# A graph network layer stack on one core: adjacency masks built by source tile and place, and the first projection by node tile

## The chip, the cores and the metric

The kernel runs on one core of a Trainium2 chip. Its time is the device time of one execution in microseconds (us). A core has a matrix engine (TensorE, PE), whose weight loads are listed apart as PEld, a vector engine (VectorE, DVE), a scalar engine (ScalarE, ACT), a general engine (GpSimd, POOL) and SyncE (SP), which here only starts transfers. Each engine runs its own instructions in their order and waits on semaphores for the others.

## The reference

1250 nodes with 768 features and 40000 edges, sorted by destination. Two layers; each adds a graph network, a linear attention and a feed-forward block to x. Cut to what this case touches:

```python
edge_index = jnp.stack([src, dst])
xn = _layernorm(x, axis=-1)
x = x + _L0_gnn_ref(xn, edge_index, ...) + _L0_mix_ref(xn[None], ...)[0]     # first layer
# in _L0_gnn_ref, gat_layer, 8 heads of 96, then 1 head of 768
h = (x @ W).reshape(n, heads, out_c)
e = leaky_relu(al_s[src] + al_d[dst], 0.2)            # softmax per destination over its edges
out = segment_sum(h[src] * alpha[:, :, None], dst)
# in _L1_gnn_ref, per convolution
deg = segment_sum(ew, col) + 1.0
norm = rsqrt(deg)[row] * ew * rsqrt(deg)[col]
agg = segment_sum(norm[:, None] * x[row], col)
```

The kernel holds the graph as two dense matrices with the source node on partitions (ten tiles of 125 nodes) and the destination node along a row: `CT` counts the edges from source to destination, and `WA` sums their weights, with ones on its diagonal.

## The kernel before

**Building the adjacency.** The edges lie 128 to a column, 313 columns. Since they are sorted by destination, eight columns (a block, 1024 edges) fall into a window of `WIN` = 38 destinations. For each of the `NB` = 40 blocks VectorE writes a mask of destinations (`destinations`, L1709: a 128x304 comparison, eight columns of 38; L1715: three products of it with the thirds of the edge weight, which is split into three bf16 numbers), the window numbers of the next block (`next_block`, L1728), and for seven of the eight columns a mask of all 1250 sources (`sources`, L1724, a 128x1250 comparison in fp16). ScalarE makes the eighth column's mask by two activations (`source`, L1344, L1346). TensorE multiplies (L906): for each column ten matmuls, one a source tile, of 152 columns (four kinds, count and three weight thirds, by 38). Blocks alternate between two halves of PSUM. ScalarE copies a finished block to SBUF (`stage_block`, L1356, L1358), and GpSimd adds it into `CT` and `WA` (`unstage`, L765 to L772, four 125x380 additions). The position of the window is read from memory into a register (`value_load`). Should an edge lie outside its window, another branch runs (`flag`); the data of this case never takes it.

**Ahead of it** GpSimd fills constants, clears `CT` (L747) and `WA` (L748), and sets the diagonal (L751). VectorE turns the edge numbers into floats (L1662), splits the weights and finds the windows (L1666 to L1703).

**After it** comes a stretch whose order counts for this change:

- VectorE: all statistics of the first LayerNorm (`layer_norm`, L1753), one addition, a wait for ScalarE's square root (L1378), then ten 125x768 normalisations (L1765), each counted on `ln_xn`.
- TensorE: the turns of all ten tiles (`transposes`, L947), then the projection `h1` of all ten (`token_major`, L955, 24 matmuls a tile), the degrees (`deg`, L989), the turned counts (`neg`, L998), then the projections `mk` and `mv` of the attention (L955 again).
- ScalarE: copies the ten turned tiles and then the ten of `h1` out of PSUM (L1335).
- SP: waits for all ten `ln_xn`, loads W2 (L533), waits for the adjacency (`adj_all`), writes `WA` to HBM (L586, L587), waits for `deg_sum`, then loads further weights.
- GpSimd: waits until `WA` is in HBM (`spill`), then sums its ten tiles in place (L786) and counts `deg_sum`, for which TensorE waits ahead of `deg`.
- VectorE, after the LayerNorm: the attention logits of each `h1` tile (`logits`, L1823, L1827), the degrees (L1867), thirty evacuations of `neg` (L1876), and during `mk` and `mv` the feature maps and segment maxima.

**Then** TensorE turns the softmax shifts (`gT`, packet `("gT", 1)`, L980), GpSimd sends them through HBM to all partitions (`drow`, L800, L782), ScalarE takes exponentials of them (`exponentials`, L1452, L1453), VectorE weighs them (`weigh`), and TensorE aggregates (L1055). Twelve query products (`query`, L972) of the attention are worked in between, three of them directly behind `gT`.

The order is written out by hand; `make_plan` numbers the PSUM packets (`take`, `give`, `emptied`), which go round four slots.

## Time and profile before

| | us |
|---|---|
| median of three runs | 3043.74 |
| the three runs | 3042.24, 3043.74, 3043.88 |
| the profiled execution | 3041.95 |
| its span | 3040.2 |
| TensorE busy in the span | 2772.0 (91%) |
| VectorE busy | 1598.3 (53%) |
| ScalarE busy | 949.1 (31%) |
| GpSimd busy | 326.5 (11%) |

All times in the rows are counted from the start of the span; 1.75 us of the profiled execution lie around it. TensorE's clock is given as the granted share of 2.4 GHz: 1.00 is 2.4 GHz, 0.50 is 1.2 GHz.

### The profile page before, as it was taken

Reading aid. Unit: us, or ns where it says so; the run is one execution under the profiler, and the core shown is the slowest. Engines: PE = TensorE matmul, PEld = TensorE weight load, DVE = VectorE, ACT = ScalarE, POOL = GpSimd, SP = SyncE. Lnnn points to the kernel's source line nnn. Section 1 sums busy time; section 2 is a strip of 40 time slices with the busy share of each in tenths; the row PEclk is TensorE's granted clock in tenths of the full one; section 3 lists DMA queues with packets and bytes.
Section 4 is the critical chain, followed back from the end, with each engine's and each line's share of the span. In section 5 each row is a group of like instructions: output and inputs, shape, how many; then the busy total and the mean of one; then the engine's idle time right before and its main releaser. Section 6 shows DMA issues by size and latency. Waiting matters only on the chain.

```text
span 3040.2 us, 33707 instructions
## 1 busy us (share of the span) xinstructions
PE 2772.0 (91%) x13517; PEld 1947.5 (64%) x13517; DVE 1598.3 (53%) x2213; ACT 949.1 (31%) x1081; POOL 326.5 (11%) x315
## 2 busy tenths in 40 slices
PE   4777799999989989969994999999799999899999
PEld 4777665578886656657772675556477777555555
DVE  8999788979994264421115211023376767322220
ACT  3666410048771142211111111013344444322210
POOL 5666330000000001100003000000000000000000
PEclk9999999999999999989996999999899999999999
DMA  9800232121103301177765610000201010200000
GB/s 244 290 0 0 81 80 71 67 83 50 35 18 67 71 23 31 53 245 249 268 230 112 126 52 16 31 0 14 69 28 28 28 42 16 109 10 11 11 11 10
DMA packets 123620, 226.61 MB, mean 75 GB/s; under 512 B 18535, under 2 KB 91788, under 8 KB 123006
## 3 DMA queue, kind: packets, MB, share of 16 engines
q1 hardware_dynamic: 107746, 178.79, 19.8%
q0 software_dynamic: 15760, 46.20, 4.9%
q8 instruction: 84, 1.38, 0.2%
q14 instruction: 30, 0.25, 0.0%
HBM read 158.92 MB, written 66.01 MB: 74 GB/s over the span
## 4 chain that ended last, share of the span: by engine, by line
PE 73%; DVE 17%; issue 3%; DMA 3%; ACT 1%; DVEq 1%; POOL 0%; SPq 0%; ACTq 0%; POOLq 0%
PE ps L955 20%; PE ps L1323 14%; PE ps L1307 13%; DVE arena L1724 6%; PE ps L1145 4%; PE ps L1179 4%; PE ps L1191 4%; PE ps L972 3%; DVE arena L1854 2%; DVE arena L1855 2%; PE ps L1244 1%; PE ps L1055 1%; DVE arena L1823 1%; PE ps L1233 1%; PE ps L1260 1%
## 5 line engine op out<-in xcount | busy, mean ns | idle before, releaser
L955 PE MATMUL ps<-arena 128*125 128x384 f32 x2160 | 712.1, 490 | 9.6 <-issue 6.1
L955 PEld LDWEIGHTS ps<-arena 128*125 128x125 f32 x2160 | 406.4, 190 | 296.2 <-issue 18.8
L1323 PE MATMUL ps<-arena 128*125 128x384 f32 x1280 | 414.6, 487 | 14.3 <-DVE arena L2232 14.3
L1307 PE MATMUL ps<-arena 128*128 128x312 f32 (+1 forms) x1536 | 407.5, 428 | 15.0 <-DVE arena L2232 15.0
L1307 PEld LDWEIGHTS ps<-arena 128*128 128x128 f32 x1536 | 292.4, 190 | 129.9 <-issue 16.9
L1323 PEld LDWEIGHTS ps<-arena 128*125 128x125 f32 x1280 | 240.9, 188 | 187.9 <-issue 16.3
L1335 ACT ACTIVATE arena<-ps 128x750 f32<-128x750 f32 (+4 forms) x145 | 111.6, 786 | 648.5 <-PE ps L955 206.3
L906 PE MATMUL ps<-arena 128*125 128x152 bf16 x3200 | 243.4, 232 | 67.7 <-DVE arena L1724 66.8
L2232 DVE SCALAR_TENSOR_TENSOR arena<-arena 128x1250 f32<-128x1250 f32 (+1 forms) x170 | 231.4, 1383 | 114.8 <-PE ps L1307 111.2
L906 PEld LDWEIGHTS ps<-arena 128*125 128x125 f16 x3200 | 220.9, 137 | 90.1 <-DVE arena L1724 89.1
L1724 DVE TENSOR_SCALAR arena<-arena 128x1250 f16<-128x1250 f16 x280 | 218.2, 851 | 0.0
L1791 DVE SCALAR_TENSOR_TENSOR arena<-ps,arena 125x768 f32<-125x768 f32 x30 | 28.7, 956 | 352.7 <-PE ps L1323 291.7
L1055 PE MATMUL ps<-arena 125*125 125x97 f32 x1600 | 184.1, 277 | 4.8 <-DVE arena L1855 4.8
L1055 PEld LDWEIGHTS ps<-arena 125*125 125x125 f32 x1600 | 182.4, 193 | 7.7 <-DVE arena L1855 5.9
L2144 DVE TENSOR_TENSOR arena<-ps,arena 128x768 f32<-128x768 f32 x34 | 32.6, 958 | 269.5 <-PE ps L1191 269.5
L1847 DVE CUSTOM_DVE_ANT_0 arena<-arena 125x1250 bf16<-125x1250 bf16 x90 | 131.4, 1460 | 23.8 <-DMA arena<-al_src 21.2
L972 PE MATMUL ps<-arena 128*128 128x312 f32 (+5 forms) x496 | 137.0, 436 | 2.1 <-ACT arena L1335 1.1
L1145 PE MATMUL ps<-arena 125*125 125x385 f32 (+1 forms) x400 | 135.3, 494 | 2.8 <-DVE arena L2039 2.8
L1179 PE MATMUL ps<-arena 128*128 128x256 f32 x612 | 134.9, 379 | 1.1 <-ACT arena L1335 1.1
L1191 PE MATMUL ps<-arena 128*128 128x384 f32 x408 | 134.5, 486 | 0.8 <-ACT arena L1335 0.8
L1179 PEld LDWEIGHTS ps<-arena 128*128 128x128 f32 x612 | 116.2, 190 | 20.6 <-issue 1.5
L1452 ACT ACTIVATE arena<-arena,small 125x1250 f32<-125x1250 f32 x80 | 106.8, 1335 | 56.1 <-DVE arena L1855 28.7
(313 smaller groups left out, 2894.5 us busy)
## 6 DMA issues: line engine op xcount, KB each, us to landing
arena<-in_L_ffn_W_dram SPq DMA_DIRECT2D x34, 1152.0 KB, 6.6
xs_rows<-arena SPq DMA_DIRECT2D x1, 30720.0 KB, 100.2
arena<-xs_rows SPq DMA_DIRECT2D x17, 768.0 KB, 7.8
y_rows<-arena POOLq DMA_DIRECT2D x34, 384.0 KB, 3.1
arena<-in_kw_dram SPq DMA_DIRECT2D x24, 512.0 KB, 5.3
arena<-al_dst POOLq DMA_DIRECT2D x18, 625.0 KB, 5.1
arena<-in_kw_dram SPq DMA_DIRECT2D x6, 1536.0 KB, 9.9
arena<-in_x_dram SPq DMA_DIRECT2D x2, 3600.0 KB
```

The lines of the kernel that those rows point to most:

```text
L906: mm = pe.matmul(bank(par, j // 3)[:, o:o + KINDS * WIN], oh_src[:, s, j * TILE:j * TILE + TILE], oh_dst[:, par, u, :, :], start=(fresh an ...
L955: mm = pe.matmul(slot(g)[0:TILE, 512 * half:512 * half + HALF], xt[:, k, i * TILE:i * TILE + TILE], w[:, k, :], start=(k == 0), stop=(k == ...
L972: mm = pe.matmul(slot(g)[0:rows, 512 * b:512 * b + w], stat, mov[:, lo + b * w:lo + b * w + w], start=(t == 0), stop=(t == len(terms) - 1))
L1055: mm = pe.matmul(slot(g)[0:TILE, 512 * (j // 5) + 97 * (j % 5):512 * (j // 5) + 97 * (j % 5) + 97], AT[m % AHEAD][:, j * TILE:j * TILE + T ...
L1145: mm = pe.matmul(slot(g)[0:TILE, 512 * b:512 * b + w], AT2[i][:, j * TILE:j * TILE + TILE], H769[:, i, lo:lo + w], start=(i == 0), stop=(i ...
L1179: mm = pe.matmul(slot(g)[:, 0:TAU], w1s[t % 2][:, k, f * P:f * P + P], xsT[t % 2][:, k, :], start=(k == 0), stop=(k == KT - 1))
L1191: mm = pe.matmul(slot(g)[:, 512 * b:512 * b + HALF], hTt[t % 2][:, f, h * P:h * P + P], w2s[t % 2][:, f, b * HALF:b * HALF + HALF], start= ...
L1307: mm = pe.matmul(slot(g)[:, 512 * b:512 * b + wd_], w[:, r % 2, ORDER[p], o * P:o * P + P], feat[place(f)][:, lo + b * wd_:lo + b * wd_ + ...
L1323: mm = pe.matmul(slot(g)[0:TILE, 512 * b:512 * b + HALF], fv[:, q, :], w2c[m][q][:, b * HALF:b * HALF + HALF], start=(p == 0 and q == 0), ...
L1724: dve.tensor_scalar(oh_src[:, u % RING, :], iota_src, src_c[:, bass.ds(col + u, 1)], None, ALU.is_equal).then_inc(ev("src_hot"), 1)
L1847: chain(dve.tensor_tensor_reduce(out=scratch, in0=neg[:, j, :], in1=row[0:TILE], scale=1.0, scalar=-3.0e38, op0=ALU.add, op1=ALU.max, accu ...
L2232: return dve.scalar_tensor_tensor(out=out_, in0=in_, scalar=edge, in1=of, op0=op, op1=ALU.mult)
```

## The change

**The adjacency.** A source number is split into its tile (`group`, 0 to 9) and its place in it (`member`, 0 to 124). The two masks are now one of 125 places and one of `SPOTS` = 380 spots (tile times 38 plus the offset of the destination in its window). For each block of eight columns VectorE compares the places (128x8x125), multiplies the mask by the first weight third, adds the block before the last from PSUM into `CT` and `WA` (`add_block`, two 125x10x38 additions), and compares the spots (eight 128x380 comparisons). ScalarE multiplies the place mask by the other two thirds (16 activations of 128x125, the weight as scale). TensorE runs four matmuls of 380 columns a column of edges, 32 a block, where it ran 80 of 152. Blocks go round four parts of PSUM. GpSimd has no part in it. The clearing of `WA` goes from GpSimd to ScalarE.

**The stretch after it** goes by node tile: VectorE's statistics and normalisation of one tile follow each other; TensorE turns tile i and then projects tile i-1; ScalarE takes root and turn of tile i+1, then copies `h1` of tile i. SP's and GpSimd's orders stay.

**The shifts.** `gT` is turned behind the first query product, ahead of the second and third.

```diff
-    transposes("xn")
-    token_major("h1", ("gW1", 0), ("gW1", 1))
+    a, b = piece("gW1", 0), piece("gW1", 1)
+    for i in range(NT):
+        packet("T", "xn", i)
+        if i >= 1:
+            packet("h1", i - 1)
+    packet("h1", NT - 1)
...
             own.step(pool.memset(ct_r[0:TILE, 0:6400], 0.0))
-            own.step(pool.memset(aa_r[0:TILE, :], 0.0))
             own.settle()
+            pool.wait_ge(ev("zeroed"), 1)
             for i in range(NT):
                 own.step(pool.tensor_copy(WA[:, i, i * TILE:i * TILE + TILE], ident[0:TILE, 0:TILE]))
             own.settle()
...
+                for u in range(SPREAD):
+                    pe.wait_ge(ev("hot"), n * SPREAD + (u + 1))
+                    pe.wait_ge(ev("hot_act"), n * SPREAD + (u + 1))
+                    for k in range(KINDS):
+                        mm = pe.matmul(bank(s, min(k, 1)), oh_src[:, par, u, k, :], oh_spot[:, par, u, :],
+                                       start=(fresh and u == 0 and k < 2), stop=False, skip_group_check=True)
                     mm.then_inc(ev("tiles_done"), 1)
...
-            transposes("xn", H, "ln_xn")
-            token_major("h1", xT, ("gW1", 0), ("gW1", 1), after="xn")
+            for i in range(NT + 1):
+                if i < NT:
+                    pe.wait_ge(ev("ln_xn"), i + 1)
+                    g = take_slot("T", "xn", i)
+                    for k in range(KT):
...
+                        mm = pe.transpose(o, H[:, i, k * P:k * P + P], ident[0:TILE, 0:TILE])
+                    ready(mm)
+                if i >= 1:
+                    emptied(pe, "T", "xn", i - 1)
+                    token_tile("h1", i - 1, xT, a, b)
...
-            for u in range(3):
-                query(u)
+            query(0)
+            pe.wait_ge(ev("gD"), 1)
+            turned_rows(("gT", 1), NT * HEADS, gD1.rearrange("p t h -> p (t h)"), gD2.rearrange("p t h -> p (t h)"))
+            query(1)
+            query(2)
...
+            act.wait_ge(ev("raw_filled"), 1)
+            act.activation(aa_r[0:TILE, :], onesc[0:TILE].broadcast_to([TILE, R_AA]), ACT.Copy, scale=0.0)\
+               .then_inc(ev("zeroed"), 1)
...
+            def weighted(par, col, n):
+
+                act.wait_ge(ev("plain"), n + 1)
+                for u in range(SPREAD):
+                    for k in range(1, 3):
+                        ins = act.activation(oh_src[:, par, u, 1 + k, :], oh_src[:, par, u, 0, :], ACT.Copy,
+                                             scale=w_p[k][:, bass.ds(col + u, 1)])
+                    ins.then_inc(ev("hot_act"), 1)
...
-            root()
             act.wait_ge(ev("xs_zero"), 16)
             act.wait_ge(ev("adj_all"), 1)
-            transposed("xn")
-            for i in range(NT):
+            root_of(0)
+            turned_tile("xn", 0, xT)
+            for i in range(NT):
+                if i + 1 < NT:
+                    root_of(i + 1)
+                    turned_tile("xn", i + 1, xT)
                 g = take(act, "h1", i)
...
+            for k in range(3):
+                chain(dve.tensor_copy(w_16, w_f))
+                chain(dve.tensor_copy(w_p[k], w_16))
+                if k < 2:
+                    chain(dve.tensor_tensor(w_f, w_f, w_p[k], ALU.subtract))
+            chain(dve.tensor_scalar(group, src_c, 1.0 / TILE, 0.5 / TILE - 0.5, ALU.mult, ALU.add))
+            chain(dve.tensor_scalar(group, group, WHOLE, None, ALU.add))
+            chain(dve.tensor_scalar(group, group, -WHOLE, None, ALU.add))
+            chain(dve.scalar_tensor_tensor(out=member, in0=group, scalar=-float(TILE), in1=src_c,
+                                           op0=ALU.mult, op1=ALU.add))
...
+            def sources(par, col, n, done):
+
+                dve.wait_ge(ev("tiles_done"), done + CREDIT)
+                dve.tensor_tensor(oh_src[:, par, :, 0, :], within.unsqueeze(1).broadcast_to(wide),
+                                  member[:, bass.ds(col, SPREAD)].unsqueeze(2).broadcast_to(wide), ALU.is_equal)\
+                   .then_inc(ev("plain"), 1)
+                dve.wait_ge(ev("plain"), n + 1)
+                dve.tensor_tensor(oh_src[:, par, :, 1, :], oh_src[:, par, :, 0, :],
+                                  w_p[0][:, bass.ds(col, SPREAD)].unsqueeze(2).broadcast_to(wide), ALU.mult)
...
+                for u in range(SPREAD):
+                    dve.tensor_scalar(oh_spot[:, par, u, :], spots, spot(u), None, ALU.is_equal).then_inc(ev("hot"), 1)
...
+                dve.tensor_tensor(CT[:, :, c], v[:, 0], CT[:, :, c], ALU.add).then_inc(ev("counted"), 1)
+                dve.wait_ge(ev("added"), b + 4)
+                dve.tensor_tensor(WA[:, :, c], v[:, 1], WA[:, :, c], ALU.add).then_inc(ev("added"), 1)
...
-            layer_norm("xn", acc, H, free=(ev("staged"), 2 * NB + 4))
+            for i in range(NT):
+                normal("xn", i, statistics(i, acc), acc, H)
```

TensorE between the adjacency and the degrees, in before, where the last two turns (L947) meet the first projection (L955, two rows).

```order
L947 MATMUL ps<-small,arena 128x125 [waits slot_free0,ev_ln_xn]
L947 MATMUL ps<-small,arena 128x125 x5
L947 MATMUL ps<-small,arena 128x125 [waits slot_free1,ev_ln_xn]
L947 MATMUL ps<-small,arena 128x125 x5
L955 MATMUL ps<-arena 125x384 [waits slot_free0,slot_free2,piece_in1,piece_in0]
L955 MATMUL ps<-arena 125x384 x11
```

The same stretch in the changed kernel, where L967 is the turn and L931 the projection.

```order
L967 MATMUL ps<-small,arena 128x125 [waits piece_in1,ev_ln_xn,piece_in0,ev_adj_all]
L967 MATMUL ps<-small,arena 128x125 x5
L967 MATMUL ps<-small,arena 128x125 [waits ev_ln_xn]
L967 MATMUL ps<-small,arena 128x125 x5
L931 MATMUL ps<-arena 125x384 [waits slot_free0]
L931 MATMUL ps<-arena 125x384 x11
L967 MATMUL ps<-small,arena 128x125 [waits ev_ln_xn]
L967 MATMUL ps<-small,arena 128x125 x5
```

A turn, which waits for `ln_xn`, now stands between any two projections.

ScalarE behind the adjacency, in before: one root (L1378), ten copies of turned tiles and ten of `h1` (both L1335).

```order
L1378 ACT_TABLE_LOAD
L1378 ACTIVATE small<-small 125x10 [waits ev_var]
L1335 ACTIVATE arena<-ps 128x6x125 [waits packet_ready,ev_adj_all,ev_xs_zero]
L1335 ACTIVATE arena<-ps 128x6x125 [waits packet_ready] x9
L1335 ACTIVATE arena<-ps 125x8x96 [waits packet_ready] x10
```

The same in the changed kernel: L1361 is the root, 128x6x125 a turned tile, 125x8x96 a tile of `h1`.

```order
L1361 ACT_TABLE_LOAD [waits ev_var,ev_adj_all]
L1361 ACTIVATE small<-small 125x1 [waits ev_xs_zero]
L1321 ACTIVATE arena<-ps 128x6x125 [waits packet_ready]
L1361 ACTIVATE small<-small 125x1 [waits ev_var]
L1321 ACTIVATE arena<-ps 128x6x125 [waits packet_ready]
L1321 ACTIVATE arena<-ps 125x8x96 [waits packet_ready]
L1361 ACTIVATE small<-small 125x1 [waits ev_var]
L1321 ACTIVATE arena<-ps 128x6x125 [waits packet_ready]
```

The root of tile 2 now stands behind the copy of tile 0 of `h1`, and so on for each tile.

TensorE at the end of `mv`, in before: L980 turns the shifts, L972 is a query.

```order
L1008 MATMUL ps<-arena 128x129 x5
L980 MATMUL ps<-small 80x125 [waits slot_free0,ev_gD]
L980 MATMUL ps<-small 80x125
L972 MATMUL ps<-arena 128x312 [waits slot_free1,piece_in0]
L972 MATMUL ps<-arena 128x312 x11
```

The same in the changed kernel, with L956 for the shifts and L948 for a query.

```order
L994 MATMUL ps<-arena 128x129 x5
L948 MATMUL ps<-arena 128x312 [waits slot_free0,piece_in0]
L948 MATMUL ps<-arena 128x312 x11
L956 MATMUL ps<-small 80x125 [waits slot_free1,ev_gD]
L956 MATMUL ps<-small 80x125
```

One query stands ahead of the shifts.

## Rows read from the trace of the kernel before

**Rows 1.** Page, part 1: busy time and share of each engine.

```profile
PE 2772.0 (91%) x13517; PEld 1947.5 (64%) x13517; DVE 1598.3 (53%) x2213; ACT 949.1 (31%) x1081; POOL 326.5 (11%) x315
```

**Rows 2.** Groups of instructions, 36 to 341 us: count, busy, mean ns, idle before them.

```profile
L906 PE MATMUL ps<-arena 128*125 128x152 bf16 x3176 | 241.6, 232 | 67.4 <-DVE arena L1724 66.4
...
L1724 DVE TENSOR_SCALAR arena<-arena 128x1250 f16<-128x1250 f16 x280 | 218.2, 851 | 0.0
...
L768 POOL TENSOR_TENSOR arena<-arena 125x380 f32<-125x380 f32 x39 | 48.0, 1231 | 0.0
```

**Rows 3.** Timeline, first block: start us, us taken, engine, line, count.

```profile
35.20 0.48 DVE L1709 TENSOR_TENSOR arena<-arena 128x304 bf16<-128x304 f32 x1 [1.45 <-issue]
35.81 1.25 DVE L1715 TENSOR_TENSOR arena<-arena 128x304 bf16<-128x304 bf16 x3
36.98 0.24 DVE L1728 TENSOR_SCALAR arena<-arena 128x38 f32<-128x38 f32 x1
37.12 3.27 DVE L1724 TENSOR_SCALAR arena<-arena 128x1250 f16<-128x1250 f16 x7
```

**Rows 4.** Timeline, 0 to 36 us, VectorE and GpSimd.

```profile
7.20 14.74 DVE L1662 CAST arena<-arena 128x384 f32<-128x384 int32 x2 [7.20 <-DMA arena<-in_edge_weight_dram]
...
10.74 10.98 POOL L748 MEMSET arena<- 125x12800 f32 x1
...
27.02 0.56 DVE L1673 TENSOR_TENSOR arena<-arena 128x384 f32<-128x384 f32 x1
```

**Rows 5.** Timeline, 341 to 455 us, all engines.

```profile
341.64 9.29 DVE L1753 BATCH_NORM_STATS2 small<-arena 125x6 f32<-125x384 f32 x20
...
341.78 1.53 PE L906 MATMUL ps<-arena 128*125 128x152 bf16 x20 [0.33 <-DVE arena L1724]
...
352.06 0.21 ACT L1378 ACTIVATE small<-small 125x10 f32<-125x10 f32 x1 [5.92 <-DVE small L1758]
...
353.38 9.17 PE L947 MATMUL ps<-small,arena 125*128 125x125 f32 x60 [10.07 <-DVE arena L1765]
354.99 0.80 ACT L1335 ACTIVATE arena<-ps 128x750 f32<-128x750 f32 x1 [2.72 <-PE ps L947]
...
358.98 0.55 SPq L586 DMA_DIRECT2D spill_w<-arena  x1
...
362.39 77.57 PE L955 MATMUL ps<-arena 128*125 128x384 f32 x240
370.33 0.81 ACT L1335 ACTIVATE arena<-ps 125x768 f32<-125x768 f32 x1 [6.70 <-PE ps L955]
...
402.76 27.37 POOL L786 TENSOR_TENSOR arena<-arena 125x6400 f32<-125x6400 f32 x4 [53.70 <-DMA spill_w<-arena]
...
439.79 2.24 PE L989 MATMUL ps<-small,arena 125*125 125x1 f32 x20
...
445.15 8.87 PE L998 MATMUL ps<-small,arena 125*125 125x125 f16 x90 [2.48 <-DVE small L1867]
...
454.31 16.04 PE L955 MATMUL ps<-arena 128*125 128x384 f32 x49
```

**Rows 6.** Prices: a timeline of ScalarE, and a group of the page.

```profile
2756.64 1.69 ACT L1632 ACTIVATE arena<-arena,small 128x250 f32<-128x250 f32 x4 [9.54 <-DVE arena L2232]
...
L2144 DVE TENSOR_TENSOR arena<-ps,arena 128x768 f32<-128x768 f32 x34 | 32.6, 958 | 269.5 <-PE ps L1191 269.5
```

**Rows 7.** Windows: us, busy by engine, then granted clock, DMA share, GB/s.

```profile
353.00:358.00 5.00, 4.62 (x23) 4.65 (x24) 5.00 (x10) 2.20 (x3) 0.00 (x0) 0.50 0.00 2
...
905.00:911.00 6.00, 3.63 (x34) 3.47 (x32) 5.84 (x8) 4.01 (x5) 0.00 (x0) 1.00 0.00 0
911.00:915.00 4.00, 3.96 (x21) 3.97 (x22) 3.88 (x4) 1.50 (x3) 0.00 (x0) 0.58 0.00 0
```

**Rows 8.** Timeline, 606 to 662 us: queries on TensorE, first exponential on ScalarE.

```profile
631.40 19.09 PE L972 MATMUL ps<-arena 128*128 128x312 f32 x72
...
644.69 1.34 ACT L1452 ACTIVATE arena<-arena,small 125x1250 f32<-125x1250 f32 x1 [6.10 <-DMA arena<-al_dst]
```

279 lines of the change are left out of this document (125 added, 154 removed).

## The prediction

> **What bounds the kernel now.** I read the shares of the page first, then the groups of the adjacency, then the timelines around it. TensorE is busy 91% of the span [rows 1], and behind the adjacency nearly all of its time is projection work that the change leaves alone. In the adjacency it is another matter: there TensorE idles 67.4 us, nearly all of it for VectorE's source masks (L1724), and VectorE has no idle time at all [rows 2]. So VectorE sets the pace. The first block shows what it needs undisturbed: 35.20 to 40.39, or 5.2 us [rows 3]. The mean of L1724 is 0.851 us [rows 2], but seven of them took 3.27 in the first block, 0.467 each [rows 3]; GpSimd's additions start later and hold VectorE up. The stretch from the first mask (35.20) [rows 3] to the end of the last adjacency matmul (341.78 + 1.53 = 343.31) [rows 5] is 308.1 us, or 7.7 a block. So most of 2.5 us a block is GpSimd's doing. Behind the adjacency TensorE is the bound again, but with a side branch beside it: WA goes to HBM (358.98), GpSimd sums it (402.76 to 430.13), and TensorE takes up the degrees only at 439.79 [rows 5]. That branch has 9.7 us to spare.
>
> **Start: -8.3 us.** Two casts of VectorE took 14.74 us from 7.20 on, since GpSimd was clearing memory until 21.72 [rows 4]. The second clearing (10.98 us) goes to ScalarE, which is idle there; an activation of 12800 columns at the 0.85 us per 1000 columns worked out below is 10.9 us and ends near 15, before anybody needs it. The casts then end with the first clearing, near 10.7, not 21.9: -11.2. Against it VectorE gets nine small instructions more and loses two (384 columns, at most 0.56 us each [rows 4]): +2.9. The masks begin at 26.9. The Trainium skill (SBUF — State Buffer, section "SBUF: two separate sides") says that VectorE and GpSimd share a port pair as an exclusive lock for a whole instruction; the two casts that end with GpSimd's clearings agree.
>
> **A block of the adjacency: 5.5 us.** *VectorE.* A comparison of 304 columns takes 0.61 us until its product starts, a product 0.39 (1.17 for three) [rows 3]. From 304 columns in 0.48 us [rows 3] to 768 in 0.958 [rows 6] is 1.03 ns a column; 696 columns more are 0.72. So the place mask costs 1.33 and its product 1.11. An addition of 380 columns from PSUM costs 0.958 - 388 x 1.03 ns = 0.56, or 0.46 if it overlaps the next by 0.1 as L1724's do; two make 0.92 to 1.12. A spot comparison lies between 0.14 (L1728 to L1724, 38 columns) and 0.467 (1250 columns) [rows 3]; in proportion to its columns it is 0.23, eight make 1.84. Sum 5.2 to 5.4. The register load of the window's place runs beside the product. *TensorE.* 32 matmuls of 380 columns. 240 f32 matmuls of 384 columns took 77.57 us, 0.323 each [rows 5]; 20 bf16 ones of 152 took 1.53, at most 0.077 each, and less the pipeline's length (0.23 [rows 2]) 0.068 [rows 5]. Half the f32 price is 0.160, the bf16 price by columns 0.171: 5.1 to 5.5 us. *ScalarE.* 16 activations of 125 columns with a scale from memory. Four of 250 columns took 1.69 us, of which the last about 0.49: 0.40 each [rows 6]. From 0.49 at 250 columns to 1.34 at 1250 [rows 8] is 0.85 ns a column; 125 fewer give 0.29 each, 4.7 us a block (6.4, if narrower were no cheaper). The three engines work on different blocks, two mask buffers deep, so the slowest decides. I take 5.5: VectorE's 5.3 and something for each waiting for the others. 40 blocks are 220 us; the first two lack the additions (-1.9), and TensorE ends 3.7 behind VectorE. Together 221.8 in place of 308.1: **-86.3 us**.
>
> **From the last adjacency matmul to `mk`: +73.5 us.** Today `mk` starts at 454.31, 111.0 us behind that matmul [rows 5]. Now I count from the matmul's end. The last two additions with their register load take 2.1 (the load 0 to 1.45, as the issue gap ahead of the first mask [rows 3]); two statistics at 0.46 [rows 5] and two small steps 1.5; a table load ahead of the root, which now waits for the variance, about 1.3 (before, it fitted into the 5.92 us ahead of L1378 [rows 5]); from root to first turn 1.3 (352.06 to 353.38 [rows 5]). First turn: 6.2. The second needs ScalarE's copy of the first (1.6 later, 0.8 long [rows 5]) and again 1.3: 9.9. The projection of tile 0 starts at 10.9 and takes 7.76 (77.57 / 10) and some 2.3 more at the half clock that TensorE had until 358 after its idle time [rows 7]: ends 21.0.
>
> Then the new order bites. Turn i+2 waits for LayerNorm i+2, this for root i+2, and this stands on ScalarE behind the copy of `h1` tile i. So TensorE waits after each projection: the copy 0.81 [rows 5] and a start of 0.2, then root to turn 1.3: 2.3 us, where before it ran on. With a turn of 0.6 a tile is 10.7. Such a gap can also cost clock: TensorE was busy 3.63 of the 6 us from 905 on, and the clock fell to 0.58 in the next four [rows 7], some 1.7 us of work lost. I charge a third of that: 11.2 a tile. [...] These rows show one such fall, no series.
>
> Seven tiles later, at 99.4, projection 7 is done, and the last LayerNorm at 102.3. Only now SP goes past its wait for ten `ln_xn`: behind that wait stand W2 and then the writing of WA. Before, SP reached it at 358.98, 15.7 behind the adjacency [rows 5]. The path then is: 44.2 until WA is out (the normalisations' end near 358.6 to 402.76), GpSimd's sums 27.4, or about 26 as VectorE's logits are over by then, and 12.0 from degrees to `mk` (439.79 to 454.31 less 2.48 of waiting for VectorE [rows 5]): 184.5. TensorE has finished `h1` near 118 and idles some 54 us for `deg_sum`. VectorE's ten logits (3.7 us each) end near 140 and hold nobody up. 184.5 - 111.0 = +73.5. The side branch with 9.7 us to spare becomes the path.
>
> **The shifts: +6.6 us.** VectorE has the shifts ready 7.6 us before TensorE turns them, so a query in front only delays them. A query is 6.36 us (19.09 / 3) [rows 8], and ScalarE's copy of it stands in front too. Behind the shifts are two trips through HBM until 644.69 [rows 8], while TensorE has queries until 650.5 only; the first aggregation comes later by the whole amount, and TensorE has more work than VectorE afterwards, so nothing gives it back. If the trips had slack it would be 0.
>
> **The sum.** -8.3 - 86.3 + 73.5 + 6.6 = -14.5. 3041.95 - 14.5 = 3027.5; the median of the runs lies 1.8 above the profiled execution, so 3029 us.
>
> **Rivals.**
> - *Narrow instructions cost more than their columns (slower).* Place: VectorE's eight spot comparisons, each with its register instruction. For it: 0.467 is the only price of such a comparison in a loop; against it: L1728 at 0.14. The kernel is slower from a block of 5.87 us, that is 0.30 a comparison; at 0.467 a block is 7.2, +68: 3095. A middling case, 6.1 a block, gives 3053. ScalarE at 0.40 (6.4 us a block) would do the same: 3065. Together 20%.
> - *The write of WA is not on the path (much faster).* If roots and LayerNorms ran ahead, `h1` would end near 95 and `mk` start near 110: -95, 2949. Against it stands the order of ScalarE word for word; between the two, with `deg_sum` in time but the waits in place, some 2975. 5%.
> - *The blocks are good, and the gaps too:* block 5.2, no clock lost, load free: 5.2 gives -12, the clock -4: 3013. This is the lower part of the forecast.
> - *Nothing moves.* A block of 5.75 to 6.0 brings it within 6 us of today. 15%.
>
> **How the numbers follow.** The forecast's own case (3013 to 3037) has 60%, a time within 0.2% (6 us, about what a measurement of this kernel can tell from no change) 15%, slower 20%, far faster 5%. The range leaves out the far faster case and the upper half of the slower one: 3008 to 3056.
>
> **What would show it.** Right: GpSimd absent from the adjacency and VectorE's spot comparisons near 0.23; a block near 5.5; nine gaps of TensorE ahead of the turns, the later ones of 2 to 2.5 us; SP's write of WA some 100 us behind the last adjacency matmul; TensorE idle some 50 us ahead of the degrees, for `deg_sum`; the first exponential of the aggregation 13.3 + 6.6 us behind the end of `mv`. Wrong: a block over 5.9, or degrees that follow `h1` at once.

## The result and the profile after

The changed kernel took 3016.7 us (median of four runs, 3016.03 to 3018.27) where the kernel before took 3043.81 in the same runs. The ratio is 0.9911, with a 95% interval of 0.9899 to 0.9924: 27 us, or 0.9%, faster. The forecast was 3029 us, its range 3008 to 3056. The profiled execution took 3017.21 us, its span is 3015.4.

Little of this shows in the shares of the page. TensorE is busy 91% as before; VectorE fell by 120 us and GpSimd by 196 [rows 1]:

```profile
PE 2751.3 (91%) x11597; PEld 1903.8 (63%) x11597; DVE 1478.4 (49%) x2248; ACT 961.8 (32%) x1552; POOL 130.1 (4%) x153
```

So I cut the two traces at the same places and set the stretches side by side. All times are from the profiled executions.

| stretch | before | after | measured | forecast |
|---|---|---|---|---|
| start to the first mask | 35.20 | 26.33 | -8.9 | -8.3 |
| first mask to the end of the last adjacency matmul | 308.1 | 219.9 | -88.2 | -86.3 |
| from there to `mk` | 111.0 | 180.7 | +69.7 | +73.5 |
| `mk` to the end of the last product behind `mv` | 177.0 | 176.6 | -0.4 | 0 |
| from there to the first exponential | 13.3 | 16.7 | +3.4 | +6.6 |
| from there to the end | 2395.5 | 2395.1 | -0.4 | 0 |
| span | 3040.2 | 3015.4 | -24.8 | -14.5 |

**The start.** Timeline of the changed kernel, start and length in us. ScalarE's clearing of `WA` (L1325) lies beside everything, and VectorE's casts (L1643) end half a microsecond behind GpSimd's one clearing (10.09), at 10.6 in place of 21.9 [rows 4]:

```profile
2.25 10.87 ACT L1325 ACTIVATE arena<-small 125x12800 f32<-125x12800 f32 x1
...
7.04 3.53 DVE L1643 CAST arena<-arena 128x384 f32<-128x384 int32 x2 [6.90 <-DMA arena<-in_edge_weight_dram]
...
26.33 1.21 DVE L1696 TENSOR_TENSOR arena<-arena 128x1000 bf16<-128x1000 f16 x1 [1.05 <-issue]
```

**The adjacency.** Groups of the stretch from 26 to 300 us (count, busy, mean ns, idle before them); they answer to [rows 2]:

```profile
L885 PE MATMUL ps<-arena 128*125 128x380 bf16 x1280 | 212.5, 327 | 10.3 <-DVE arena L1706 10.3
...
L1706 DVE TENSOR_SCALAR arena<-arena 128x380 bf16<-128x380 f16 x320 | 76.6, 314 | 0.0
L1700 DVE TENSOR_TENSOR arena<-arena 128x1000 bf16<-128x1000 bf16 x40 | 48.0, 1200 | 5.3
L1696 DVE TENSOR_TENSOR arena<-arena 128x1000 bf16<-128x1000 f16 x40 | 47.9, 1198 | 3.0 <-PE ps L885 1.9 <-issue 1.1
...
L1714 DVE TENSOR_TENSOR arena<-ps,arena 125x380 f32 x40 | 22.0, 550 | 10.0 <-issue 6.3 <-PE ps L885 3.7
```

TensorE idles 10.3 us where it idled 67.4. VectorE idles 18.3 us, but only 5.6 of them for TensorE; 6.3 stand ahead of the first addition (L1714) without a wait that the profile shows. The two are nearly level. The blocks are not alike, though. One of the earlier blocks on VectorE, and one of the later ones (place mask L1696, product L1700, first addition L1714; the second and the eight spot comparisons are left out):

```profile
92.81 1.20 DVE L1696 TENSOR_TENSOR arena<-arena 128x1000 bf16<-128x1000 f16 x1
94.16 1.20 DVE L1700 TENSOR_TENSOR arena<-arena 128x1000 bf16<-128x1000 bf16 x1
...
95.81 0.56 DVE L1714 TENSOR_TENSOR arena<-ps,arena 125x380 f32 x1 [0.45 <-issue]
...
98.57 1.20 DVE L1696 TENSOR_TENSOR arena<-arena 128x1000 bf16<-128x1000 f16 x1
```

```profile
190.24 1.20 DVE L1696 TENSOR_TENSOR arena<-arena 128x1000 bf16<-128x1000 f16 x1
191.58 1.20 DVE L1700 TENSOR_TENSOR arena<-arena 128x1000 bf16<-128x1000 bf16 x1
...
192.69 0.55 DVE L1714 TENSOR_TENSOR arena<-ps,arena 125x380 f32 x1
...
195.45 1.20 DVE L1696 TENSOR_TENSOR arena<-arena 128x1000 bf16<-128x1000 f16 x1
```

The earlier block takes 5.76 us, the later one 5.21. The whole difference lies between the product and the first addition, where the register load of the window's place stands. The 15 blocks that start between 47.1 and 127.3 take about 5.7 us (5.61 to 5.76), the twenty from 132.9 on 5.21.

**The stretch behind it.** Timeline on all engines. L967 is a turn, L931 the projection, L1361 the root, L1801 the normalisation, L768 GpSimd's sums, L975 the degrees. It answers to [rows 5]:

```profile
244.78 1.45 PE L885 MATMUL ps<-arena 128*125 128x380 bf16 x8
...
252.29 1.48 PE L967 MATMUL ps<-small,arena 125*128 125x125 f32 x6 [6.06 <-DVE arena L1801]
...
256.96 8.82 PE L931 MATMUL ps<-arena 128*125 128x384 f32 x24
...
288.53 0.81 ACT L1321 ACTIVATE arena<-ps 125x768 f32<-125x768 f32 x1 [6.95 <-PE ps L931]
289.24 0.19 ACT L1361 ACTIVATE small<-small 125x1 f32<-125x1 f32 x1
...
289.66 0.68 DVE L1801 TENSOR_SCALAR arena<-arena,small 125x768 f32<-125x768 f32 x1
...
290.40 0.86 PE L967 MATMUL ps<-small,arena 125*128 125x125 f32 x6 [1.91 <-DVE arena L1801]
...
291.10 7.91 PE L931 MATMUL ps<-arena 128*125 128x384 f32 x24
...
343.31 0.55 SPq L594 DMA_DIRECT2D spill_w<-arena  x1
...
387.55 25.21 POOL L768 TENSOR_TENSOR arena<-arena 125x6400 f32<-125x6400 f32 x4 [370.97 <-DMA spill_w<-arena]
...
412.81 4.36 PE L975 MATMUL ps<-small,arena 125*125 125x1 f32 x20 [51.85 <-POOL arena L768]
...
426.92 77.64 PE L931 MATMUL ps<-arena 128*125 128x384 f32 x240
```

Read it from the end. `mk` starts at 426.92, the degrees at 412.81, and TensorE had idled 51.85 us for GpSimd's sums. These began at 387.55, 44.2 us behind the issue of the write of `WA` (343.31), and that stood behind the tenth normalisation. Each normalisation in turn stood behind ScalarE's copy of `h1` (288.53, then the root at 289.24), which gives the wait of 1.91 us ahead of the turn.

**The shifts.** The timeline of the changed kernel behind `mv` (L994 is the product, L948 a query, L956 the turn of the shifts, L782 and L764 their trip, L1430 the first exponential):

```profile
600.69 2.84 PE L994 MATMUL ps<-arena 125*128 125x129 f32 x24
...
603.37 6.47 PE L948 MATMUL ps<-arena 128*128 128x312 f32 x24
609.67 0.38 PE L956 MATMUL ps<-small 125*80 125x125 f32 x2
...
611.12 1.20 POOL L782 DMA_DIRECT2D al_dst<-arena  x2 [45.26 <-ACT arena L1321]
...
613.91 2.18 POOL L764 DMA_DIRECT2D arena<-al_dst  x4 [1.59 <-DMA al_dst<-arena]
...
620.27 1.34 ACT L1430 ACTIVATE arena<-arena,small 125x1250 f32<-125x1250 f32 x1 [9.45 <-DMA arena<-al_dst]
```

The turn comes one query later, but the trip from GpSimd's issue to the exponential takes 9.15 us, where it took 12.4 before (632.27 to 644.69; the exponential is in [rows 8]).

### The profile page after: what moved, and what is told of

It is laid out like the page before. It is cut to its first block, busy times and chain, and to the rows that moved or that the text cites. A ratio compares the mean times of both kernels' runs of the same rounds, so it can differ in the third digit from the quotient of the medians.

```text
span 3015.4 us, 30384 instructions
## 1 busy us (share of the span) xinstructions
PE 2751.3 (91%) x11597; PEld 1903.8 (63%) x11597; DVE 1478.4 (49%) x2248; ACT 961.8 (32%) x1552; POOL 130.1 (4%) x153
## 4 chain that ended last, share of the span: by engine, by line
PE 79%; DVE 11%; DMA 4%; issue 2%; ACT 2%; POOL 1%; DVEq 1%; SPq 0%; ACTq 0%; POOLq 0%
PE ps L931 21%; PE ps L1309 14%; PE ps L1293 14%; PE ps L1165 4%; PE ps L1131 4%; PE ps L1177 4%; PE ps L885 4%; PE ps L948 3%; DVE arena L1874 2%; DVE arena L1875 2%; DMA spill_w<-arena 1%; PE ps L1230 1%; PE ps L1041 1%; PE ps L1219 1%; DVE arena L1706 1%
## 5 line engine op out<-in xcount | busy, mean ns | idle before, releaser
L931 PE MATMUL ps<-arena 128*125 128x384 f32 x2160 | 715.7, 492 | 9.5 <-issue 5.8
L931 PEld LDWEIGHTS ps<-arena 128*125 128x125 f32 x2160 | 406.8, 190 | 295.2 <-issue 20.9
L885 PE MATMUL ps<-arena 128*125 128x380 bf16 x1280 | 212.5, 327 | 10.3 <-DVE arena L1706 10.3
L885 PEld LDWEIGHTS ps<-arena 128*125 128x125 bf16 x1280 | 172.6, 137 | 49.9 <-DVE arena L1706 13.0
L1335 ACT ACTIVATE arena<-arena 128x125 bf16<-128x125 bf16 x640 | 189.6, 386 | 40.5 <-DVE arena L1696 40.5
L1041 PE MATMUL ps<-arena 125*125 125x97 f32 x1600 | 187.6, 280 | 5.4 <-DVE arena L1875 5.4
L1041 PEld LDWEIGHTS ps<-arena 125*125 125x125 f32 x1600 | 186.1, 196 | 8.3 <-DVE arena L1875 5.5
L948 PE MATMUL ps<-arena 128*128 128x312 f32 (+5 forms) x496 | 137.3, 436 | 4.2 <-DVE arena L1837 2.1
L1430 ACT ACTIVATE arena<-arena,small 125x1250 f32<-125x1250 f32 x80 | 106.8, 1335 | 60.5 <-DVE arena L1875 30.6
```

Of the source, the lines that this page charges most:

```text
L885: mm = pe.matmul(bank(s, min(k, 1)), oh_src[:, par, u, k, :], oh_spot[:, par, u, :], start=(fresh and u == 0 and k < 2), stop=False, skip_ ...
L931: mm = pe.matmul(slot(g)[0:TILE, 512 * half:512 * half + HALF], xt[:, k, i * TILE:i * TILE + TILE], w[:, k, :], start=(k == 0), stop=(k == ...
L948: mm = pe.matmul(slot(g)[0:rows, 512 * b:512 * b + w], stat, mov[:, lo + b * w:lo + b * w + w], start=(t == 0), stop=(t == len(terms) - 1))
L1041: mm = pe.matmul(slot(g)[0:TILE, 512 * (j // 5) + 97 * (j % 5):512 * (j // 5) + 97 * (j % 5) + 97], AT[m % AHEAD][:, j * TILE:j * TILE + T ...
L1335: ins = act.activation(oh_src[:, par, u, 1 + k, :], oh_src[:, par, u, 0, :], ACT.Copy, scale=w_p[k][:, bass.ds(col + u, 1)])
```

## The experiments

My theory was: the adjacency gains since GpSimd no longer holds VectorE up; most of the gain goes back in the stretch behind it, through one chain (copy of `h1`, root, normalisation, write of `WA`, sums, degrees); and each part can be had without the other. The rivals stand with each run. One thing on precision: the stretch from the start of the last aggregation matmul (L1041 in the changed kernel) to the end is the same code in all kernels, and in the 14 profiled executions it took between 2109.7 and 2116.6 us. A single span is good to some 3 us either way, so I read small effects within their stretch. Differences to the changed kernel's 3016.7 us are between medians that were taken at different times; the kernel before, which ran beside each of them, had medians of 3043.2 to 3045.7.

### The stretch behind the adjacency as it was

```diff
-            for i in range(NT):
-                normal("xn", i, statistics(i, acc), acc, H)
+            layer_norm("xn", acc, H)
...
-            root_of(0)
-            turned_tile("xn", 0, xT)
...
+            root()
+            transposed("xn")
...
+            transposes("xn", H, "ln_xn")
```

> The changed kernel with the stretch behind the adjacency as it was before: all statistics, one root, ten normalisations, ten turns, then the ten projections. The adjacency and the shifts stay changed. Theory A (the gain of the adjacency was given back only by the order of that stretch): mk starts 111 us behind the last adjacency matmul (246.2), at 357, 70 us earlier than in the changed kernel: 2947 us. Rival B (something of the new adjacency, such as VectorE's additions at its end or the clock, lengthens the stretch too): 2955 us or more.

It took 2953.0 us (2952.0 to 2953.71), ratio 0.9698 (0.9682 to 0.9714). Its timeline (L1757 the statistics, L918 a turn, L926 a projection):

```profile
247.90 9.30 DVE L1757 BATCH_NORM_STATS2 small<-arena 125x6 f32<-125x384 f32 x20
...
261.02 8.65 PE L918 MATMUL ps<-small,arena 125*128 125x125 f32 x60 [15.05 <-DVE arena L1769]
...
361.28 11.20 PE L926 MATMUL ps<-arena 128*125 128x384 f32 x34
```

The last adjacency matmul ended at 245.97, so `mk` follows after 115.3 us, not 111.0 and not 180.7. Theory A holds for 65 of the 70 us, though the time, 2953.0, is nearer to rival B's 2955 than to theory A's 2947. Rival B is right on the remaining 4: before, the statistics began 1.7 us ahead of the end of the last matmul (341.64 against 343.31, [rows 5]), now 1.9 behind it, since VectorE first has the last two additions to make. And this kernel, with half of the change taken back, is 64 us faster than the changed one.

### Only the stretch, on the old adjacency

The same edit the other way round, in the kernel before: node tile by node tile, with the old masks and GpSimd's additions.

> The kernel before with only the stretch behind the adjacency by node tile; adjacency and shifts as before. Theory A (the loss of 69.7 us belongs to that order alone and adds to the rest): mk starts 180 us behind the last adjacency matmul in place of 111: 3043.8 + 70 = 3114 us. Rival B (it needs the new adjacency, for instance since GpSimd was free earlier): under 3095 us.

3113.55 us (3113.36 to 3116.72), ratio 1.0227 (1.0210 to 1.0244). The end of the last adjacency matmul is at 343.3 and `mk` starts at 524.96, 181.7 us behind it; TensorE waited 50.5 us for the sums there too. The loss belongs to the order alone, and the parts add up.

### The write of WA first

```diff
+            sp.wait_ge(ev("adj_all"), 1)
+            sp.dma_start(A["spill_w"][0:120], WA[0:120]).then_inc(ev("spill"), 16)
+            sp.dma_start(A["spill_w"][120:TILE], WA[120:TILE]).then_inc(ev("spill"), 16)
             sp.wait_ge(ev("ln_xn"), NT)
             load(w2f, A["L0_gnn_W2"].rearrange("(k p) n -> p k n", p=P), "w2f")
-            sp.wait_ge(ev("adj_all"), 1)
...
```

> The changed kernel, but SP writes WA to HBM as soon as the adjacency is done, and waits for the ten normalisations and loads W2 behind that. Theory A (the late write of WA is what keeps TensorE idle for 52 us): the write goes out near 249 in place of 343.3, GpSimd's sums run from about 293 to 320, long before h1 ends at 361. Then VectorE is next: its ten logits of 3.7 us start only behind the last normalisation (343) and end at 380, the degrees wait for them, mk starts near 390 in place of 426.9: 3016.7 - 37 = 2980 us. Rival B (the idle time is not the write's, another wait stands behind it): mk starts within 5 us of 427, 3012 to 3017 us.

2996.72 us (2987.93 to 2999.09), ratio 0.9836 (0.9816 to 0.9856): 20 us gained, not 37. The trace shows 15 of the missing 17 ahead of `mk`. Timeline of this kernel at 288 us:

```profile
288.31 25.46 POOL L768 TENSOR_TENSOR arena<-arena 125x6400 f32<-125x6400 f32 x4 [271.72 <-DMA spill_w<-arena]
...
289.22 13.16 DVE L1801 TENSOR_SCALAR arena<-arena,small 125x768 f32<-125x768 f32 x1
...
302.44 1.51 PE L967 MATMUL ps<-small,arena 125*128 125x125 f32 x6 [14.39 <-DVE arena L1801]
```

The write went out at 247.94 as expected, and the sums ran from 288.31 to 313.8. But a normalisation that takes 0.68 us now took 13.16: it ended when GpSimd's first sum, 6400 columns in 13.65 us (288.31 to 301.96), had ended. TensorE waited 14.39 us for it, 12.5 more than in the other tiles, and two projections behind it took 9.03 and 9.60 us in place of 7.91, at a lower clock: everything behind came about 15 us later (`mk` at 404.94, not 390). As expected, the degrees no longer wait for the sums: VectorE's ten logits, which stand behind the last normalisation, now hold TensorE between the degrees (374.59) and `mk`. The Trainium skill (SBUF — State Buffer, section "Who interferes with whom") says that VectorE's `tensor_scalar` can take a pair of ports that it shares with GpSimd, and that of two instructions that need it the second fully blocks until the first is done. The trace agrees: 13.16 us for the normalisation beside a sum of 13.65.

### The same with short sums

```diff
-                ins = pool.tensor_tensor(WA[:, 0:n, :], WA[:, 0:n, :], WA[:, lo:lo + n, :], ALU.add)
-                if lo > 1:
-                    own.step(ins)
+                for t in range(n):
+                    ins = pool.tensor_tensor(WA[:, t, :], WA[:, t, :], WA[:, lo + t, :], ALU.add)
+                    if lo > 1:
+                        own.step(ins)
```

> As the kernel whose SP writes WA first, with each of GpSimd's sums of several tiles cut into sums of one tile (1250 or 1280 columns in place of up to 6400). There a normalisation of VectorE took 13.16 us and ended with GpSimd's first sum of 13.65 us; all of h1 came 15 us later for it. Theory A (VectorE gets its turn only between two of GpSimd's instructions): the longest normalisation is under 3 us, the last one ends near 344 again, mk starts near 391, 3016.7 - 36 = 2981 us. Rival B (VectorE waits for the whole row of GpSimd's instructions): a wait of over 10 us stays, 2993 us or more.

2992.75 us (2991.73 to 2993.90), ratio 0.9830 (0.9812 to 0.9847). By its time this is rival B; by its trace it is not. The wait of over 10 us is gone. Timeline of VectorE during GpSimd's sums (L1803 the normalisation, L1792 the statistics):

```profile
289.46 2.16 DVE L1803 TENSOR_SCALAR arena<-arena,small 125x768 f32<-125x768 f32 x1
291.54 1.01 DVE L1792 BATCH_NORM_STATS2 small<-arena 125x6 f32<-125x384 f32 x2
...
303.14 3.14 DVE L1803 TENSOR_SCALAR arena<-arena,small 125x768 f32<-125x768 f32 x1
```

Two normalisations were held up, for 1.5 and 2.5 us, and the statistics between them not at all (1.01 us, as without GpSimd). Yet the last normalisation came near 351, not 344, and `mk` at 398.31, not 391. The waits are 4 of these 7 or 8 us. TensorE's clock is the rest: the projections behind the longer waits took 9.60 and 8.96 us in place of 7.91, and one at 329.70, behind a wait of 1.90 only, took 9.60 as well. I had left the clock out.

### The root ahead of the copy

```diff
             root_of(0)
             turned_tile("xn", 0, xT)
+            root_of(1)
             for i in range(NT):
                 if i + 1 < NT:
-                    root_of(i + 1)
                     turned_tile("xn", i + 1, xT)
+                if i + 2 < NT:
+                    root_of(i + 2)
```

> The changed kernel, but ScalarE takes the root of tile i+2 ahead of the copy of h1 tile i. Theory A (each wait of TensorE for a normalisation is ScalarE's copy in front of the root, and the last wait sets the write of WA): the waits of 1.9 us ahead of turns 2 to 9 shrink to under 0.5, h1 ends near 345 in place of 361, the last normalisation comes near 321 in place of 342.9, the write of WA and with it mk come 22 us earlier: 2995 us. Rival B (VectorE's own chain of statistics, root and product is what is late): the waits stay over 1.5 us, 3015 us.

2991.79 us (2989.16 to 2992.58), ratio 0.9823 (0.9807 to 0.9839). The waits ahead of the turns are gone altogether (a turn of 0.81 us follows the projection at once, a tile takes 8.38 us in place of 10.51, and no projection but the first is longer than 7.91), the write of `WA` goes out at 319.86 in place of 343.31, and `mk` follows the adjacency after 155.2 us in place of 180.7. TensorE still idles 46.35 us for the sums. Theory A holds. The place of eight small roots in ScalarE's order is worth 25 us, since the chain from the last normalisation to the degrees is rigid.

### What sets the pace of the adjacency

Two more spot comparisons in a block, written to scratch:

```diff
+                    dve.tensor_scalar(w_f.bitcast(BF16)[:, 0:SPOTS], spots, spot(0), None, ALU.is_equal)
+                    dve.tensor_scalar(w_f.bitcast(BF16)[:, 384:384 + SPOTS], spots, spot(1), None, ALU.is_equal)\
+                       .then_inc(ev("extra"), 1)
```

> The changed kernel with two more spot comparisons in each block, written to scratch. In its trace the blocks take 5.74 us until the 30.7 MB clearing of xs_rows is over (near 131 us) and 5.21 us afterwards. Theory A (VectorE sets the pace of every block; a spot comparison costs 0.24 us): every block is 0.47 us longer, the adjacency 19 us, 3036 us. Rival B (TensorE sets the pace of the 21 later blocks, with VectorE following it): only the earlier half is longer, 9 us, and the later blocks stay under 5.4 us; 3026 us.

3034.05 us (3030.48 to 3039.35), ratio 0.9977 (0.9967 to 0.9987): 17 us more than the changed kernel. The blocks take about 6.15 and 5.67 us in place of 5.7 and 5.21. What VectorE is given to do comes through in both kinds.

Four more matmuls in a block, the first one repeated:

```diff
+                    if fresh and u == 0:
+                        for _ in range(4):
+                            pe.matmul(bank(s, 0), oh_src[:, par, u, 0, :], oh_spot[:, par, u, :],
+                                      start=True, stop=False, skip_group_check=True)
```

> The changed kernel with four more matmuls of 380 columns at the start of each block (the first one repeated), 0.164 us each. Theory A (TensorE follows VectorE closely in the early blocks, where it waits 0.33 us a block, and is full in the later ones): early blocks 0.3 us longer, later ones 0.6, together 19 us, 3036 us. Rival B (TensorE has room, VectorE alone bounds): later blocks longer by under 0.2 us, 3020 us.

3034.84 us (3031.55 to 3038.65), ratio 0.9971 (0.9962 to 0.9981): 18 us more. But the earlier blocks hardly moved (5.8 us, with their outliers), the later ones went to 5.80. So TensorE needs 5.8 us for 36 matmuls, and the 32 of the changed kernel just fit: in the later blocks both engines are full, and in the earlier ones TensorE had half a microsecond of room. The sum came out as expected, its division did not: I had put a third of it on the earlier blocks. They took 1.4 us, the twenty later ones 11.7, and the few at either end of the adjacency the other 4.6.

The register load ahead of the place mask:

```diff
                         b = bp * 4 + s
+                        at = window(b - 2)
                         sources(s % 2, b * SPREAD, b, b * SPREAD - SPREAD)
-                        add_block((s + 2) % 4, b - 2)
+                        add_block((s + 2) % 4, b - 2, at)
```

> The changed kernel, but VectorE's register load of the window's place stands ahead of the place mask of the block in place of between the product and the addition. Theory A (the early blocks are 0.53 us longer since the register load takes longer while the transfer runs, and it ends 0.4 us behind the product): the gap of 0.4 ahead of L1714 goes and does not come back elsewhere, early blocks 5.3 us, 8 to 10 us in all: 3008 us. Rival B (VectorE waits for the load wherever it stands): the gap moves ahead of the place mask, 3015 to 3022 us.

3008.25 us (3006.09 to 3011.68), ratio 0.9892 (0.9876 to 0.9909), 8.5 us less by the medians. The interval overlaps that of the changed kernel, so the trace decides: the adjacency ends at 238.09 in place of 246.23, and all blocks of the loop now take 5.21 us. VectorE in this kernel, at the place of the early block above:

```profile
94.87 1.20 DVE L1700 TENSOR_TENSOR arena<-arena 128x1000 bf16<-128x1000 bf16 x1
95.99 0.55 DVE L1718 TENSOR_TENSOR arena<-ps,arena 125x380 f32 x1
```

The gap of 0.45 us is gone. That it was the register load is shown; why it takes longer up to about 130 us is only argued. The gap goes when the clearing of `xs_rows` (30720 KB on the page, from the core's memory) ends. The weights that are read right behind it keep the DMA engines just as busy, but only for one or two blocks (133 to 143), and they do not bring it back; nor do the two blocks ahead of the loop (39.01, with no gap) show it while the clearing runs. It takes the clearing and the loop's register work together, it seems. A kernel without the clearing wasn't tried.

Last, is GpSimd the cause of the old block's length? In the kernel before, three of its four additions a block take one column of 38 (so this kernel leaves out most of the sums of `WA`):

```diff
-                pool.tensor_tensor(k[:, :, 3, :], k[:, :, 3, :], k[:, :, 2, :], ALU.add).then_inc(ev("unst_b"), 1)
+                pool.tensor_tensor(k[:, :, 3, 0:1], k[:, :, 3, 0:1], k[:, :, 2, 0:1], ALU.add).then_inc(ev("unst_b"), 1)
...
```

> The kernel before, in which three of GpSimd's four additions a block (the two into the stage and the one into WA) take one column of 38: WA is not summed. Theory A (2.5 of the 7.7 us a block are VectorE held up by GpSimd's additions, about in proportion to their time): the block falls to near 5.8, the adjacency from 308 to about 232 us, the kernel to about 2968 us. Rival B (something else, such as the 30.7 MB transfer or ScalarE's copies, holds the blocks up): the block stays over 7 us, the kernel over 3015 us.

2969.75 us (two runs), ratio 0.9762 (0.9742 to 0.9782). The blocks take 5.8 to 6.0 us in place of 7.7. Groups of this kernel, 36 to 262 us:

```profile
L907 PE MATMUL ps<-arena 128*125 128x152 bf16 x3043 | 206.5, 231 | 23.5 <-ACT arena L1347 18.0 <-DVE arena L1725 5.5
...
L1725 DVE TENSOR_SCALAR arena<-arena 128x1250 f16<-128x1250 f16 x272 | 140.0, 584 | 0.0
```

The source mask fell from 0.851 us [rows 2] to 0.584, undisturbed it is 0.467 [rows 3]. The old masks, left alone, were no dearer for VectorE than the new ones: the first block took 5.2 us in the forecast's reading, the later blocks of the changed kernel take 5.21. The last adjacency matmul ends 69.6 us earlier (273.76 in place of 343.31), where the changed adjacency is 88.2 us shorter. So some four fifths of what the change wins there it could have had by taking most of GpSimd's work away alone. The rest isn't divided by a run: one full addition a block was left on GpSimd here, and TensorE now waits for ScalarE's column (18.0 us) more than for VectorE's (5.5), a column that the change does away with.

### The shifts

```diff
-            query(0)
             pe.wait_ge(ev("gD"), 1)
             turned_rows(("gT", 1), NT * HEADS, ...)
+            query(0)
             query(1)
```

> The changed kernel with the shifts turned ahead of the first query, as before. Theory A (in the trace before, the trip of the shifts through HBM, 12.4 us from GpSimd's issue at 632.27 to the first exponential at 644.69, ran behind 2.4 MB of weights that SP had issued 3 us earlier; in the changed kernel these are nearly through by the issue at 611.12, and the trip takes 9.15): put back, the trip takes 12.4 again, and the first exponential follows the end of mv by 13.3 in place of 16.7: 3.4 us less, 3013 us. Rival B (the trip takes 9.2 us wherever it starts, and the delay of a whole query is gone): 6.6 us less, 3010 us.

3012.7 us (3012.09 to 3014.5), ratio 0.9895 (0.9877 to 0.9912). Its interval overlaps that of the changed kernel, so the time alone settles nothing; the trace does:

```profile
602.51 1.20 POOL L782 DMA_DIRECT2D al_dst<-arena  x2 [37.86 <-ACT arena L1321]
...
608.24 2.37 POOL L764 DMA_DIRECT2D arena<-al_dst  x4 [4.53 <-DMA al_dst<-arena]
...
614.65 1.34 ACT L1430 ACTIVATE arena<-arena,small 125x1250 f32<-125x1250 f32 x1 [5.81 <-DMA arena<-al_dst]
```

The first half of the trip (602.51 to 608.24) takes 5.7 us again, where the changed kernel had 2.8 (611.12 to 613.91). The whole trip is 12.1, and the exponential follows the end of `mv` by 13.1: 3.7 us less. Theory A. (SP had issued the same weights at 598.94 and 599.35, 3 us ahead of the trip; in the changed kernel at 600.88 and 601.30, 10 us ahead.)

### Versions that beat both

Two kernels put the pieces together. The first has the old stretch behind the adjacency, the register load ahead, the shifts in front, and SP's two weight loads behind the first half of the shifts' trip:

```diff
-            for key in order[5:10]:
+            for key in order[5:7]:
+                send(key)
+            sp.wait_ge(ev("gD_out"), 32)
+            for key in order[7:10]:
                 send(key)
```

> The new adjacency with the register load ahead of the place mask, the stretch behind it as before, the shifts ahead of the first query, and SP's two weight loads (2.4 MB) behind the first trip of the shifts. Theory A (the parts add up): 2953.0 - 8.5 for the register load - 3.4 for the shifts - 3.3 for a trip of 9.2 us = 2938 us. Rival B (TensorE has so much query work behind mv that an earlier shift brings nothing, and the weights come too late for query 6): 2944 us.

2944.67 us (2939.52 to 2949.06), ratio 0.9666 (0.9647 to 0.9685). This is the number of rival B, but the trace shows another reason for half of what is missing from theory A's 2938: the trip was not shorter by its 3.3 us. The other half is smaller than the spread of these four runs.

```profile
533.20 1.20 POOL L780 DMA_DIRECT2D al_dst<-arena  x2 [38.41 <-ACT arena L1312]
535.73 0.37 SPq L578 DMA_DIRECT2D arena<-in_mixT_dram  x1
536.00 2.18 POOL L762 DMA_DIRECT2D arena<-al_dst  x4 [1.59 <-DMA al_dst<-arena]
...
545.65 1.34 ACT L1418 ACTIVATE arena<-arena,small 125x1250 f32<-125x1250 f32 x1 [6.12 <-DMA arena<-al_dst]
```

Its first half takes 2.8 us, but now the weights run beside the second half, which takes 9.65 (536.00 to 545.65) in place of 6.4. The sum is 12.45 as before. I had moved the collision, not removed it. Five kernels with the weights at three places agree on this, but none was run without the weights nearby.

The second goes by node tile, but with the roots ahead, `WA` first, short sums, and VectorE's logits of tile i-3 behind normalisation i:

> As the kernel just ahead of it, but by node tile, with the root of tile i+2 ahead of the copy of h1 tile i, SP writing WA first, GpSimd's sums one tile at a time, and VectorE's logits of tile i-3 behind normalisation i. Theory A (the order by node tile gains the 8 us by which the first projection starts earlier, once neither the write of WA nor the logits stand behind all normalisations): h1 ends 95 us behind the adjacency, mk starts 110 us behind it in place of 115, 2933 us. Rival B (GpSimd's sums now run beside the normalisations and cost VectorE, and TensorE behind it, more than that): over 2938 us.

2941.06 us (2936.70 to 2943.96), ratio 0.9663 (0.9645 to 0.9682). From the last adjacency matmul to `mk` it takes 114.1 us (238.15 to 352.29), against 117.2 in the first version (238.62 to 355.86) and 115.3 in the whole-stretch kernel. The first projection starts 10.8 us behind the adjacency (248.96) instead of 24. Some 12 of these 13 us go again by the end of the tenth: eight turns now stand between the projections (5 us), the first and the eighth projection run partly at the lower clock (9.01 and 9.28 us in place of 7.91), and beside GpSimd's short sums VectorE's logits products take 3.63 us each in place of 0.95 and two normalisations 2.34 in place of 0.68, for which TensorE waits 3.8 us in all, up to 3.0 ahead of one turn. Rival B names the mechanism rightly, though it costs the gain and not more than that. By the times the two versions can't be told apart. Both are 2.4 to 2.5% faster than the changed kernel, and the order by node tile is worth some 3 us once the roots, the write of `WA` and the logits no longer stand in its way.

## Why the prediction was right, point by point

**The start** (-8.9, forecast -8.3) and **the bound before** (VectorE, held up by GpSimd) are right, the latter now shown by the kernel with thin additions.

**The block.** The mean, 219.9 / 40, is the 5.5 us of the forecast, and the parts are close, each from its start to the start of the next in a later block: place mask 1.34 (1.33), product 1.11 (1.11), the two additions 0.93 together (0.92 to 1.12), a spot comparison 0.23 (0.23), a matmul 0.164 (0.160 to 0.171), ScalarE 4.75 (4.7). Sizing by columns between the two nearest rows worked here; the rival with 0.30 to 0.47 a comparison did not come true. But the 5.5 is a mean of 5.7 and 5.21, and the step "the register load runs beside the product" is wrong for the earlier blocks: the load costs half a microsecond in each, 8 us in all. What I had added for the engines' waiting for each other covered it by luck: the mean is right for a reason that I did not have.

**The stretch.** Each link measured: first turn 6.06 us behind the matmul (forecast 6.2), first projection 10.7 (10.9) and its end 19.6 (21.0), wait ahead of a turn 1.9 (2.3), last normalisation 96.6 (102.3), then 44.7 for the write (44.2), 25.2 for the sums (26), 14.1 from degrees to `mk` (12.0). TensorE idled 51.85 us (54). The 5.7 us up to the last normalisation come from small terms. The wait was 1.9: the copy starts at once, the root 0.1 us before it is through, and the turn 1.16 behind the root in place of 1.3. I counted a turn of 0.6 ahead of the last normalisation, which doesn't wait for it. The first projection took 8.8 us, not 10.1. And I charged a third of 1.7 us in each of seven tiles for the clock, where it fell once in them (9.60 us for the second projection, in place of 7.91). Windows of the changed kernel (us, busy by engine, granted clock, DMA share, GB/s) show it, and they show where the clock did cost, at the degrees after the long idle time:

```profile
268.40:278.00 9.60, 9.59 (x26) 5.14 (x24) 0.53 (x3) 0.80 (x1) 0.00 (x0) 0.82 0.00 0
278.00:342.00 64.00, 51.61 (x180) 30.09 (x180) 12.81 (x37) 11.09 (x20) 0.00 (x0) 1.00 0.00 1
...
412.80:417.00 4.20, 4.19 (x20) 4.19 (x21) 0.00 (x0) 0.00 (x0) 0.00 (x0) 0.50 0.65 146
```

Six waits of 1.9 us in a row left the clock at 2.4 GHz. Yet it fell again behind the ninth (9.60 us for the projection at 343.62), where the path no longer ran through it. The other kernels with these waits alone show the same: one or two of ten projections at 9.6 us behind waits of 1.9, and none where the projections ran without waits (the kernel before, the whole-stretch kernel, and the one with the roots ahead from its second projection on). So such a wait can cost clock, and mostly doesn't; which one does isn't explained here. The Trainium skill (TensorE: Matmul & The Clock Gate, section "HAM oscillation — how this bites in real kernels") tells of a loop whose work in each step was shorter than its wait, and which started every step at the lower clock, and of larger ones, with work far longer than the wait, that kept the higher. With 8.6 us of work to 1.9 of wait this loop is near the second kind, but not free of falls. At 1.2 GHz the degrees took 4.36 us, not the 2.24 of [rows 5]; that is the 2.1 us by which the last link was longer.

**The shifts** (+3.4, forecast +6.6) is the term that was mis-sized most. The step that failed is that I took the trip's length as fixed. It had run behind SP's weights, and a later start found them gone. The delay by a query was right: GpSimd's issue stands 7.6 us behind the end of `mv` in place of 0.9, 6.7 us more (forecast 6.6). The trip that follows was 3.3 us shorter (9.15 in place of 12.4).

**The sum.** The stretches came to -24.8 where I had -14.5: 0.6 from the start, 1.9 from the blocks, 3.8 from the stretch, 3.2 from the shifts, 0.8 from places with no forecast. Another 2.3 us are the median, which lies 0.5 below the profiled execution and not 1.8 above it. All of these went the same way, which put the result into the lower part of the forecast's own case. The gain itself, 27 us, is nearly twice the 15 that I forecast: it is what is left between -97 and +73, so errors of a few per cent in the large terms make a large one in it. One of the rivals' sums has a slip: the far faster case (2949) leaves out the +6.6 of the shifts, and with it is 2955; the whole-stretch kernel, which is that case by another edit, took 2953.0.

## What to carry to other kernels

Before an order is changed, follow what stands behind the last step of the old order on every queue: here a DMA behind a wait for all ten normalisations turned a finer pipeline into 70 us of loss, and nothing in the reordered engines' own orders shows that. When a gain is far below what the bound promises (here 27 us of 97), look for the stretch that gave it back and undo that half alone. A bulk transfer issued just ahead of a short one lengthened it here from 2.8 to 5.7 us; moving either only helps if they then don't meet elsewhere.

## What the runs showed of the hardware

- A VectorE normalisation (125x768, scalar operands) stood still for a whole GpSimd addition of 6400 columns, 13.16 in place of 0.68 us. So did a pair of the logits' products with two inputs from the core's memory in the kernel before (15.33 us in place of 1.83, see the row below), while a pair of reductions (1.81 us) and the statistics (1.01 us) kept their lengths beside the same additions. So in these traces it depends on the instruction, and not only on whether GpSimd works. Cutting the addition into pieces of 1280 columns cut the wait to 1.5 to 2.5 us and did not lengthen the sums as a whole much (26.6 against 25.5 us).

Timeline of VectorE in the kernel before, during GpSimd's sums:

```profile
402.20 15.33 DVE L1823 TENSOR_TENSOR arena<-arena 125x768 f32<-125x768 f32 x2 [4.07 <-ACT arena L1335]
417.56 1.81 DVE L1827 TENSOR_REDUCE small<-arena 125x8 f32<-125x768 f32 x2
```

- A register load on VectorE was hidden under a product of 1.20 us in the later blocks and stood out by 0.4 to 0.45 us while 30720 KB were written out of the core's memory. Reads that kept the DMA engines as busy for the next one or two blocks did not do this.
- The first half of the shifts' trip through HBM took 5.7 us when 2.4 MB of weights had been issued 3 us earlier, and 2.8 when they had been issued 10 us earlier or stood behind it.
- A wait of 1.9 us ahead of each of nine turns lowered TensorE's clock behind two of them in the changed kernel (9.60 us for a projection of 7.91); without the waits no projection behind the first was lengthened.
